# Grouped score matmuls and quarter-tile masks in a fused decoder layer

## The reference, cut to what matters

```python
q_lr = jnp.einsum('bhtd,hdr->bhtr', q, Wq_lsr)
k_lr = jnp.einsum('bhtd,hdr->bhtr', k, Wk_lsr)
scores = jnp.einsum('bhir,bhjr->bhij', q_lr, k_lr) * scale
scores = jnp.where(causal_mask, jnp.float32(-jnp.inf), scores)
attn = jax.nn.softmax(scores, axis=-1)
y = jnp.einsum('bhij,bhjd->bhid', attn, v)
...
x = _layernorm(x + _L0_attn_ref(x, ...), axis=-1)
x = _layernorm(x + _L0_xattn_ref(x, ctx_1024, mask_S2_ik0, ...), axis=-1)
x = _layernorm(x + _L0_ffn_ref(x, ...), axis=-1)
```

## Time and profile before

| | |
|---|---|
| median of 3 runs | 1116.73 us (1114.6 to 1124.2) |
| the profiled execution | 1121.9 us, span of its instructions 1120.2 us |
| PE busy | 1014.2 us (91% of the span) |
| PEld busy | 797.8 us (71%) |
| DVE busy | 735.5 us (66%) |
| ACT busy | 621.8 us (56%) |
| POOL busy | 281.9 us (25%) |
| DMA queue of SP | 53.8% of 16 engines' span |
| mean granted clock of PE | 0.958 of full speed |

### The profile page before, as it was taken

The page is one execution under the profiler, slowest core; times in us unless marked ns, Lnnn a source line. Parts: engine busy times, 40 slices in busy tenths (PEclk is TensorE's granted clock), DMA queues, the critical chain, the costliest instruction groups (busy, mean ns, idle before and its releaser), DMA issues.

```text
span 1120.2 us, 24734 instructions
## 1 busy us (share of the span) xinstructions
PE 1014.2 (91%) x9124; PEld 797.8 (71%) x9188; DVE 735.5 (66%) x1565; ACT 621.8 (56%) x1185; POOL 281.9 (25%) x537
## 2 busy tenths in 40 slices
PE   4559899999999999999999999999999999999863
PEld 4346677777777777777777777777777777777652
DVE  5334577777676777677776777677677776776443
ACT  1123455666565565666565565666555666665642
POOL 5000122222222222222222222222222222222222
PEclk8668999999999999999999999999899999999986
DMA  7564656664655566654655566755555666552000
GB/s 185 91 115 95 118 85 126 129 127 106 105 111 116 94 117 129 128 121 103 113 111 116 93 118 128 130 117 107 100 111 92 118 129 129 122 106 44 21 10 19
DMA packets 114786, 118.61 MB, mean 106 GB/s; under 512 B 20649, under 2 KB 98283, under 8 KB 114667
## 3 DMA queue, kind: packets, MB, share of 16 engines
q1 hardware_dynamic: 114667, 117.03, 53.8%
HBM read 74.00 MB, written 41.94 MB: 104 GB/s over the span
## 4 chain that ended last, share of the span: by engine, by line
PE 62%; DMA 15%; SPq 7%; issue 6%; DVE 5%; ACT 3%; POOL 2%; ACTq 0%; DVEq 0%; POOLq 0%
PE ps_m L477 13%; PE ps_m L469 10%; DMA parts_dram<-parts 10%; PE ps_o L547 6%; PE ps_s L495 6%; PE ps_t L495 5%; SPq L353 5%; DMA stack<-parts_dram 4%; PE ps_s L506 3%; PE ps_t L506 3%; PE ps_m L440 2%; DVE row_max L871 2%; PE ps_m L449 2%; PE ps_m L603 2%; PE ps_m L640 2%
## 5 line engine op out<-in xcount | busy, mean ns | idle before, releaser
L668 ACT ACTIVATE p<-ps_t 128x1024 f32<-128x1024 f32 x192 | 196.5, 1024 | 137.0 <-PE ps_t L501 122.0
L871 DVE TENSOR_REDUCE row_max<-ps_s 128x4 f32<-128x1024 f32 (+1 forms) x192 | 232.7, 1212 | 35.3 <-PE ps_s L501 23.0
L1064 POOL TENSOR_TENSOR var<-mv,eps 128x2 f32<-128x2 f32 x96 | 18.8, 196 | 620.4 <-DVE mv L894 620.4
L495 PE MATMUL ps_s<-stack 48*128 48x128 f32 (+1 forms) x1024 | 109.4, 313 | 42.5 <-DMA stack<-parts_dram 30.1
L495 PEld LDWEIGHTS ps_s<-stack 48*128 48x128 f32 x1024 | 73.5, 191 | 76.5 <-DMA stack<-parts_dram 27.9
L693 ACT COPY yu<-ps_o 128x512 f32<-128x512 f32 x64 | 37.5, 586 | 138.9 <-PE ps_o L547 138.9
L495 PEld LDWEIGHTS ps_t<-stack 50*128 50x128 f32 x1024 | 72.8, 189 | 58.2 <-issue 36.3
L495 PE MATMUL ps_t<-stack 50*128 50x128 f32 (+1 forms) x1024 | 108.4, 311 | 5.4 <-DMA stack<-shift_parts 2.5
L547 PE MATMUL ps_o<-p,v_pad 128*32 128x256 f32 (+1 forms) x2048 | 98.0, 333 | 0.0
L547 PEld LDWEIGHTS ps_o<-p,v_pad 128*32 128x32 f32 x2048 | 58.5, 111 | 40.0 <-issue 18.5
L1090 POOL TENSOR_TENSOR xr_lo<-dx,xr_hi 128x512 fp32r<-128x512 f32 x32 | 40.8, 1274 | 143.0 <-ACT xr_hi L749 143.0
(11 more groups left out here) (170 smaller groups left out, 2819.7 us busy)
## 6 DMA issues: line engine op xcount, KB each, us to landing
stack<-parts_dram SPq DMA_DIRECT2D x384, 128.0 KB, 4.4
parts_dram<-parts SPq DMA_DIRECT2D x64, 512.0 KB, 5.1
x_in<-in_x_turned SPq DMA_DIRECT2D x32, 256.0 KB, 2.9
x_res<-in_x SPq DMA_DIRECT2D x32, 256.0 KB, 3.2
out_x<-sum SPq DMA_DIRECT2D x64, 128.0 KB, 1.8
ctxT<-in_ctx_turned SPq DMA_DIRECT2D x32, 120.0 KB, 5.7
stack<-shift_parts SPq DMA_DIRECT2D x128, 8.0 KB
p<-in_Wq SPq DMA_DIRECT2D x1, 256.0 KB, 2.7
```

What stands on the lines that cost most here:

```text
L495: nc.tensor.matmul(o, left[b.slot][r0:r0 + rows_n, h // 2, rows_at:rows_at + P], right[b.slot][r0:r0 + rows_n, h // 2, col:col + width], s ...
L668: nc.scalar.activation(p[c][:], ps_t[:], ACT.Exp).then_inc(exp_done[c], 1)
L871: nc.vector.tensor_reduce(row_max[:, tile, :, j0:j0 + nj], ps_s[:].rearrange("p (g j w) -> p g j w", j=nj, g=2), AX_X, ALU.max) \
```

## The change

At each position the chunks of both kinds are now issued one behind the other (`slot(c)`), and only then both masks. A mask is added by four matmuls of 64x64 instead of two of 128x128: two PSUM banks (`half`, which is also the half of the array's rows) times two halves of the output's partitions (`block`). The mask tiles hold both blocks and are twice as large, and POOL fills each in two pieces of 64 partitions. The query projection, which stood between S2 and T2, stands behind T2 and both masks.

```diff
-        mask_s = sb("mask_s", [P, 4, P], BF16)
-        mask_t = sb("mask_t", [P, 4, P], BF16)
+        mask_s = sb("mask_s", [P, 2, 4, P], BF16)
+        mask_t = sb("mask_t", [P, 2, 4, P], BF16)
...
+            def causal_mask(c, target, mask, first):
+
+                for block in range(2):
+                    for half in range(2):
+                        r = slice(64 * half, 64 * half + 64)
+                        o = target[64 * block:64 * block + 64, half * 512:(half + 1) * 512]
+                        if c in NARROW:
+                            o = o.rearrange("p (n w) -> p n w", n=4)
+                        else:
+                            o = o.rearrange("p (n w) -> p n w", n=2)[:, :, first:first + P]
+                        last = nc.tensor.matmul(o, identb[r, 64 * half:64 * half + 64], mask[r, block, 0:o.shape[1], :],
                                                 start=False, stop=True, skip_group_check=True)
...
-                def Tr(c):
+                        wait(pe, max_done[prev], count)
+                        chunk_scores(Sb, c, ps_s, stack[0], stack[1])
                     if on[PROBS]:
                         if c == T_ORDER[0]:
                             pe.wait_ge(shift_loaded[Pb.slot], Pb.dma_count(4))
                         prev, count = before(T_ORDER, c, Pb)
-                        scores(Pb, c, ps_t, exp_done[prev], count, t_filled, stack[1], stack[0], mask_t)
+                        wait(pe, exp_done[prev], count)
+                        chunk_scores(Pb, c, ps_t, stack[1], stack[0])
+                    if on[SCORES]:
+                        causal_mask(c, ps_s, mask_s, P).then_inc(s_filled, 1)
+                    if on[PROBS]:
+                        causal_mask(c, ps_t, mask_t, 0).then_inc(t_filled, 1)
...
-                S(2)
+                slot(2)
                 if on[IN]:
                     bank = bank_free(pe, "q", at)
                     pe.wait_ge(v_["xT_lo"], A.n + 1)
                     rows_out_split(bank, "Wq", xT[A.slot]).then_inc(filled["f_q"], 1)
-                Tr(2)
...
+            for half in range(2):
+                r = slice(64 * half, 64 * half + 64)
+                for m, sign in ((mask_s, 1), (mask_t, -1)):
+                    link(g.affine_select(out=m[r], in_=m[r], compare_op=ALU.is_ge, fill=MASKED, base=0,
+                                         pattern=[[64 * sign, 2], [0, 4], [-sign, P]], channel_multiplier=sign))
```

More of the change, by code:

```diff
@@ L479, in tokens_out_split, with chunk_scores @@
                 return last
-            def scores(b, c, target, free, free_count, done, left, right, mask):
-                wait(pe, free, free_count)
+            def chunk_scores(b, c, target, left, right):
                 heads = chunk_heads(c)
@@ L488, in scores @@
                 width, col = (P, rows_at) if c in NARROW else (T, 0)
+                rows_n = STACK_ROWS if left is stack[1] else ONES_ROW
                 for h in heads:
@@ L491, in scores @@
                     at_h = column(c, h)
[L492 to L495, removed]
+                    nc.tensor.matmul(target[:, at_h:at_h + width],
+                                     left[b.slot][r0:r0 + rows_n, h // 2, rows_at:rows_at + P],
                                      right[b.slot][r0:r0 + rows_n, h // 2, col:col + width],
[L497 to L501, removed]
-                                                start=False, stop=True, skip_group_check=True)
[L503 to L508, removed]
+                                     start=h - heads[0] < 2, stop=False, skip_group_check=True)
+            def causal_mask(c, target, mask, first):
[8 more added lines that the diff above has]
+                        last = nc.tensor.matmul(o, identb[r, 64 * half:64 * half + 64], mask[r, block, 0:o.shape[1], :],
+                                                start=False, stop=True, skip_group_check=True)
+                return last
             def step(at):
@@ L512, in step, with slot @@
                 on = [live(at, s) for s in range(5)]
-                def S(c):
+                def slot(c):
                     if on[SCORES]:
@@ L518, in S @@
                         prev, count = before(S_ORDER, c, Sb)
-                        scores(Sb, c, ps_s, max_done[prev], count, s_filled, stack[0], stack[1], mask_s)
-                def Tr(c):
+                        wait(pe, max_done[prev], count)
+                        chunk_scores(Sb, c, ps_s, stack[0], stack[1])
                     if on[PROBS]:
@@ L559, in step @@
                     last.then_inc(filled["f_yu"], 1)
-                S(0)
-                Tr(0)
+                slot(0)
                 if on[CROSS]:
@@ L575, in step @@
                     tokens_out_split(bank, yT, "Wo").then_inc(filled["f_z1"], 1)
-                S(3)
-                Tr(3)
+                slot(3)
                 if on[FFN]:
@@ L584, in step @@
                     rows_out_split(bank, "Wk", xT[A.slot]).then_inc(filled["f_k"], 1)
-                S(1)
-                Tr(1)
+                slot(1)
                 if on[CROSS]:
@@ L594, in step @@
                     tokens_out_split(bank, xT[Sb.slot], "Wv").then_inc(filled["f_v"], 1)
-                S(4)
-                Tr(4)
+                slot(4)
                 if on[CROSS]:
@@ L609, in step @@
                     rows_out_split(bank, "Wkf", xk).then_inc(filled["f_k3"], 1)
-                S(5)
-                Tr(5)
+                slot(5)
                 if on[FFN]:
```

## The result

| | before | changed |
|---|---|---|
| median | 1117.59 us (1114.6 to 1124.2, 4 runs) | 1174.29 us (1168.91 to 1182.37, 4 runs) |
| span of the profiled execution | 1120.2 us | 1180.7 us |
| mean granted clock of PE | 0.958 | 0.892 |

The changed kernel is slower: ratio 1.0505, 95% interval 1.0427 to 1.0583.

A forecast was written before the change was run, and what follows sets the result against it. Two nearly equal loops, PE's step (31.4 us) and SP's transfers (30.7), were taken as the bound. From 1115.7: loop +16, early steps +4, start +4, end -3 give 1137; clock +12 gives the forecast of 1148 us, range 1119 to 1176.

The forecast's parts named there:

- SP's loop: Cycle from one output transfer through parts, shift rows, PE and ACT to the next; 30.7 us before, 32.0 forecast, ruling every step.
- Part A: Stretch from SP's output issue to the start of T0, only SP and DMA working; mean some 24.6 us.
- B: Stretch from T0 to the next output issue; forecast to grow by 1.23, from 6.14 to 7.37 us.
- The 1137 at full clock: Forecast time in us before any loss from PE's clock falling to its lower level.
- the end: Last two steps, with no loop behind them; forecast to give back 3 us.
- The clock: PE falling to half clock after idle stretches: one in three of 27 steps, 1.3 us each, +12 us.
- half clock in nearly every step: Rival: PE at the lower clock in nearly all steps, 27 x some 1.5 us more, 1177 us; chance 0.13.
- PE's own loop: PE's own work per step; forecast to fall from 31.4 to about 30.3 us.
- Small tiles in turn: Rival: the four mask tiles run one after another, loop of 33.3 us, 1172 us in all; chance 0.12.
- Setup: POOL's longer mask building ahead of SP's first parts transfer, forecast near 22; +4 us at the start.
- No difference: Rival: earlier landings and shorter mask tails give a step loop of 31.5 us, 1124 us in all; chance 0.17.
- faster: Rival: PE's step stays the longer loop and falls to 30.3 us, 1087 us in all; chance 0.08.

The follow-up runs named there:

- The order alone: Against the kernel before: grouped chunks and later query projection, but full-array masks of two matmuls and the short mask setup; 1144.49 us, ratio 1.0224.
- the new queue: Against the changed kernel: SP sends query parts to DRAM first and issues input, output and residual while they are on their way; 1106.13 us, ratio 0.9876.
- The tiles alone: Against the kernel before: masks of four 64x64 tiles in the old order, each behind its own chunk; 1139.75 us, ratio 1.0181.
- the extra matmuls: Against the changed kernel: useless 512-column matmuls on PE, five ahead of S0's wait and two ahead of T0's; 1140.86 us, ratio 1.0204.

## Why the prediction was right and where it was off

**SP's loop takes the lead: right.** Part A was to stay at 24.6 and measured 24.48. B was to be 7.37 and was 7.34; its parts were forecast at 2.34 and measured at 2.34, at 1.05 and measured at 1.01, at 3.98 and measured at 3.99. The order alone, the new queue and the query projection put back each moved B or removed its effect as the loop demands. (6.14 was not B's least value before: the last of the 27 steps has 5.15. Nothing hangs on it.)

The 1137 at full clock, from which the forecast starts, is right in part by luck. The loop gave 13 instead of 16 us and the start with the early steps 6.3 instead of 8, while the end took 2.7 more instead of 3 less; the errors cancel.

**The clock: right in kind, and the term that was mis-sized.** The term reads "I count one in three: 27 / 3 x 1.3 = +12". Just ahead of it the prediction says that about half of such steps fell, and it gives no reason for going below that. It was 22 of 27, and a fall cost more than 1.3: 45 / 22 = 2.0. The sum comes out when this is replaced: 1137 + 45 = 1182, against the 1182.37 us of the profiled execution, the slowest of the four runs that make the median. Two things in it were off. Falls took longer than the 3.50 of the earlier trace rows, which I had taken as their length: 6.8 in most steps, and then the whole query projection lies in one. And I judged how often it falls from idle stretches ahead of full-array masks. The changed step loses its clock after shorter waits than the step without tiles; with the order alone my +12 would have been right (12 measured). The time landed at that of the rival "half clock in nearly every step" (1177), and with 22 of 27 its condition is nearly met. That it still lies inside the range is luck.

The Trainium skill on HAM oscillation (TensorE: Matmul & The Clock Gate) has the clock low after the wait for DMA in every round of its loop. It tells this of waits of 3 to 5 us; here PE's waits for the stack were 1.4 on average without the first long one ((46.8 - 10.6) / 26), so the prediction went too far in saying that by this page the rival would be the forecast. The trace comes near its pattern in the changed kernel (22 of 27); in the order alone, with waits just as long, the clock fell in 11 of 27.

**PE's own loop: near.** 30.3 was forecast; 30.75 was measured once SP no longer set it. The saving per step is 31.41 - 30.75 = 0.66, not 1.1. My sum gave the tiles much of it, and measured by themselves they save nothing: what the masks gain, the operations behind them lose, or it lies beside waits. A wide position can take 1.01, less than the 1.13 that I forecast (timeline of PE, changed kernel):

```profile
673.60 0.50 PE L490 MATMUL ps_s<-stack 48*128 48x256 f32 x4
673.94 0.40 PE L490 MATMUL ps_t<-stack 50*128 50x256 f32 x4
674.27 0.30 PE L505 MATMUL ps_s<-mask_s,identb 64*64 64x256 bf16 x4
674.40 0.28 PE L505 MATMUL ps_t<-mask_t,identb 64*64 64x256 bf16 x4
674.61 0.33 PE L440 MATMUL ps_m<-ident,x 128*128 128x128 f32 x1
```

But it does so at half of them: with the new queue it is 1.01 at chunks 2 and 4, and mostly 1.25 to 1.28 at chunks 3 and 5, where 1.42 and 1.34 stood before.

**Small tiles in turn: wrong, as I had weighed it.** Four tiles of 512 columns take 0.41 with their tail; in turn, at the 0.22 of one matmul, they would take 0.9. The Trainium skill's restriction on column tiling (TensorEngine Tiling (Array Packing), Restrictions and Gotchas), with its load time (TensorE: Matmul & The Clock Gate, LDWEIGHTS), gave 0.053 a load and 0.21 for four in turn by my estimate. The trace has 0.10 for one load, but all four of the row at 397.37 within 0.11, because they overlap.

**Setup: right.** Four selects of 1.09 and two fills of 0.96 put SP's first `parts` at 22.21 (22 forecast); with the early steps 8 was forecast and 6.3 measured. **The end: wrong sign.** It was to give back 3 and cost 2.7. With the extra matmuls the end takes 100.1 (1136.6 - 1036.51), as before (1120.2 - 1020.19 = 100.0), and low stretches there add up to 37 us instead of 47, so these 2.7 seem to be the clock's too. The timeline of POOL and SP at the start of the changed kernel:

```profile
17.08 1.09 POOL L1054 TENSOR_SCALAR_AFFINE_SELECT mask_s<-mask_s 64x1024 bf16<-64x1024 bf16 x1
...
22.21 0.40 SPq L346 DMA_DIRECT2D parts_dram<-parts  x1
```

**No difference and faster.** The faster case needed a part A shorter than 22.9, and it was 24.48; no difference needed a loop of 31.5, and it was 31.86. Faster is what the new queue brings about: the saving on PE was real, and the loop through SP hid it.

## What to carry to other kernels

Split the step into the loops that can set it and give each its length; where two are within 1 us, ask of every moved wait on which of them it lies, since the new order saved PE 0.6 a step and cost the transfer loop 1.2 to 1.4. Where a transfer loop sets the step, look first at what its queue holds behind a wait: moving one output in SP's queue turned a loss of 5% into a gain of 1%. Once PE waits in every step, its clock is a term of its own; here it was some 40 of the 57 us. A run with extra matmuls ahead of the wait measures it.

## What the runs showed that I had not expected

- In these kernels the clock fell more often with masks of four 64x64 tiles than with full-array ones, after waits of the same length: in 8 of 9 steps against 1 of 10 in the grouped order. The tiles alone raised the steps with a fall from 2 to 9 of 27, four of them with no idle time of PE ahead of T0. In the changed kernel a fall mostly lasted 6.8, in the order alone mostly 3.4. Whether it is the size of the tiles, the shorter time that the masks keep PE busy, or where the step lies in time, was not separated.
- The loads of four 64x64 tiles overlap: four in 0.11, at 0.10 for one. And two masks of four tiles behind one another take 0.34 from 674.27 to 674.61, where the same two masks in the order alone take 0.45.
- The extra matmuls, seven of 512 columns a step, cost 0.36 a step where the wait was no longer than they were, and returned 1.65 a step where the clock had been falling in 22 of 27 steps.
